# POOL's order of gathers and roots, and two loads moved from the last stage's start into the experts' middle

## The reference

```python
x = x + cross_attention(layernorm(x), ctx, ...)          # 16 heads
x = x + moe(layernorm(x), gate, w_gate, w_up, w_down)    # 64 experts, top 8, 192 hidden
x = x + memory_attention(layernorm(x), ctx, mask)        # softmax(x3 ctx^T / sqrt(512) + mask) ctx
x = x + ffn(layernorm(x), gate_w, up_w, down_w, scales)  # 1408 hidden, ternary weights
```

## Time and profile before

| | |
|---|---|
| median of three runs | 1554.14 us |
| the profiled execution | 1556.91 us, its span 1555.2 us |
| mean granted clock | 0.948 of 2.4 GHz |
| PE busy | 1416.4 us, 91% |
| DVE busy | 1027.0 us, 66% |
| ACT busy | 890.5 us, 57% |
| POOL busy | 609.0 us, 39%, of which L1631 (G gathers) 116.8 us, 112 of them |
| DMA | 278.23 MB, mean 179 GB/s |

### The profile page before, as it was taken

How to read it: one execution, slowest core, us unless ns; L and a number is a source line. 1 busy time by engine, 2 the same in 40 slices (tenths; PEclk the granted TensorE clock), 3 DMA queues, 4 the chain that set the end, 5 groups by cost and what they waited for, 6 DMA issues and landing times.

```text
span 1555.2 us, 37426 instructions
## 1 busy us (share of the span) xinstructions
PE 1416.4 (91%) x8673; PEld 1195.1 (77%) x8674; DVE 1027.0 (66%) x2093; ACT 890.5 (57%) x2022; POOL 609.0 (39%) x698
## 2 busy tenths in 40 slices
PE   7999899999845999999999999999982599999998
PEld 6887666657724898888889888888971488888888
DVE  5555588876687676777676766766645467676742
ACT  5554599873366666666666666766631244444442
POOL 1223387761112322323332323323236566666322
PEclk9999799999955999999999999999995899999999
DMA  6221692001162788878777777777657544444200
GB/s 223 82 88 55 247 359 80 2 5 48 62 250 67 254 277 280 275 252 281 268 266 275 271 256 248 265 243 254 234 162 261 156 149 145 134 135 135 74 13 29
DMA packets 93287, 278.23 MB, mean 179 GB/s; under 512 B 12757, under 2 KB 12886, under 8 KB 92502
## 3 DMA queue, kind: packets, MB, share of 16 engines
q1 hardware_dynamic: 69526, 199.67, 36.6%
q0 software_dynamic: 23680, 77.61, 16.5%
HBM read 209.07 MB, written 76.81 MB: 184 GB/s over the span
## 4 chain that ended last, share of the span: by engine, by line
PE 41%; issue 9%; POOL 5%; DMA 4%; DVE 3%; ACT 3%; ACTq 1%; SPq 1%; DVEq 1%; POOLq 0%
PE m_g L1307 17%; PE m_y L1327 11%; PE f_g L1742 5%; DMA y_rows<-y 2%; PE m_x L1292 2%; POOL G L1631 2%; PE f_y L1757 2%; POOL hT_low L1637 2%; ACT wd_high L1076 1%; PE m_h L1315 1%; PE m_h L1316 1%; PE f_x L1715 1%; DVE X L1796 1%; PE f_sc L1701 1%; DMA raw_gu<-y_rows,slot 1%
## 5 line engine op out<-in xcount | busy, mean ns | idle before, releaser
L1235 POOL DMA_INDIRECT xg<-h_rows,idx x168 | 194.2, 1156 | 454.7 <-PE m_x L1292 445.6
L1307 PE MATMUL m_g<-wgu_high,bxTh 128*128 x660 | 235.8, 357 | 2.3 <-DVE bxTl L1378 2.0
L1307 PE MATMUL m_g<-wgu_low,bxTh 128*128 x660 | 223.3, 338 | 0.0
L1307 PE MATMUL m_g<-wgu_high,bxTl 128*128 x660 | 223.2, 338 | 0.0
L1742 PE MATMUL f_g<-x4T_high,ffn_gu 128*128 128x256 f32 x704 | 176.6, 293 | 4.7 <-DVE x4T_low L1866 4.6
L1742 PE MATMUL f_g<-x4T_low,ffn_gu 128*128 128x256 f32 x704 | 169.8, 283 | 0.0
L1081 DVE TENSOR_TENSOR wgu_low<-raw_gu,wgu_high (+1 forms) x64 | 112.6, 1759 | 85.0 <-ACT wgu_high L1071 80.3
L1378 DVE TENSOR_TENSOR bxTl<-m_x,bxTh 128x512 fp32r<-128x512 f32 x166 | 114.6, 691 | 73.7 <-ACT bxTh L1475 67.5
L1493 ACT ACTIVATE y<-m_y 128x512 f32<-128x512 f32 x164 | 98.3, 600 | 107.1 <-PE m_y L1327 78.3
L1327 PE MATMUL m_y<-wd_high,hidTm 128*128 x328 | 143.9, 439 | 5.9 <-DVE hidTm L1392 3.9
L626 POOL TENSOR_TENSOR prob<-prob,inv 128x512 f32<-128x512 f32 x128 | 130.5, 1042 | 40.1 <-DVE inv L577 38.6
(11 more groups left out here) (266 smaller groups left out, 3291.2 us busy)
## 6 DMA issues: line engine op xcount, KB each, us to landing
raw_gu<-in_exp_gu SPq DMA_DIRECT2D x64, 768.0 KB, 6.4
y_rows<-y SPq DMA_DIRECT2D x164, 256.0 KB
raw_d<-in_exp_d SPq DMA_DIRECT2D x64, 512.0 KB, 7.2
y_rows<-zero SPq DMA_DIRECT2D x64, 256.0 KB, 3.4
ffn_gu<-ffn_gu_words SPq DMA_DIRECT2D x1, 5632.0 KB, 22.0
raw_c<-in_ctxT SPq DMA_DIRECT2D x16, 256.0 KB, 2.7
X<-in_x SPq DMA_DIRECT2D x4, 1024.0 KB, 5.7
h_rows<-h SPq DMA_DIRECT2D x16, 256.0 KB, 2.0
```

Of the source, the lines that this page charges most:

```text
L1235: eng.indirect_dma_start(xg[:, u, :].bitcast(F32), None, h_dram, bass.IndirectOffsetOnAxis(ap=idx[half][:, u:u + 1], axis=0)).then_inc(s_g ...
L1307: m = eng.matmul(pg[u % 2][:, 0:2 * I], xT[l][:, u % 2, c, :], W.gu[r][:, buf * DC + c, :], start=c == 0 and n == 0, stop=c == DC - 1 and ...
```

## The change

Four edits.

1. memT of batch 0 and the mask get places in `spares` (whose other users in the last stage, `xn` and `x3T`, get space of their own) and are loaded by SP in the experts, after group 27, once DVE has ORed the last chunk of words. PE's first scores wait for memT alone, the first read for both halves of the memory.
2. In the last stage SP waits for the early addition k6_1 before it loads mem and the scales. Wdn follows as before.
3. `gather(1, ...)` waits for nothing.
4. POOL's order: three gathers of batch 1, root a of batch 0, the other thirteen, four of batch 2, root 4 of batch 0, five of batch 2, root a of batch 1. The last seven of batch 2 go behind the lows of batch 0, 2, 2, 2 and 1 behind f = 0 to 3, and then eight of batch 3 behind f = 4 to 10 (two behind 10), where there had been eight behind f = 1 to 7.

```diff
 # experts, SP
-                    each_group(eng, begin, groups, stores)
+                    done = WORDS_AT[-1] + 3
+                    with eng.Fori(begin, done) as i:
+                        stores(i)
+                    dveD.wait(eng, FC - 1, "words")
+                    apart(eng, s_apart)
+                    eng.dma_start(memT, a["memT"][:, 0, :, :]).then_inc(s_mem, 16)
+                    eng.dma_start(open8, a["mask"].unsqueeze(0).to_broadcast([P, B, S])).then_inc(s_m, 16)
+                    each_group(eng, done, groups, stores)
 # finish
+    GATHERS_2, GATHERS_3 = {0: 2, 1: 2, 2: 2, 3: 1}, {4: 1, 5: 1, 6: 1, 7: 1, 8: 1, 9: 1, 10: 2}
...
-        xn = spare[0].rearrange("p (i d) -> p i d", i=TPB)
-        x3T = spare[1].rearrange("p (i c n) -> p i c n", i=TPB, c=DC)
+        xn, x3T = sb("xn", [P, TPB, D]), sb("x3T", [P, TPB, DC, P])
 # finish, SP
-            load(0)
-            eng.dma_start(open8[:, :, :], a["mask"].unsqueeze(0).to_broadcast([P, B, S])).then_inc(s_m, 16)
+            added.wait(eng, 0, f"k{K - 2}_{TPB - 1}")
+            apart(eng, s_apart)
+            load(0, True)
 # finish, POOL
-                    if b > 0:
+                    if b > 1:
                         dveA.wait(eng, b - 1, f"k{k}_{i}")
...
-            gather(1, places[:4])
+            gather(1, places[:3])
             deviations_a(0)
-            gather(1, places[4:])
+            gather(1, places[3:])
+            gather(2, places[:4])
             deviations_4(0)
+            gather(2, places[4:9])
             deviations_a(1)
-            gather(2, places)
 
             for b in range(B):
-                n = 0
+                n, of_2, beside = 0, 9, GATHERS if b > 0 else GATHERS_3
                 for f in fs:
                     low(b, f)
+                    if b == 0:
+                        gather(2, places[of_2:of_2 + GATHERS_2.get(f, 0)])
+                        of_2 += GATHERS_2.get(f, 0)
                     if b < B - 1 and f == 7 + (b == 0):
                         deviations_4(b + 1)
                     if b < B - 3:
-                        gather(b + 3, places[n:n + GATHERS.get(f, 0)])
-                        n += GATHERS.get(f, 0)
+                        gather(b + 3, places[n:n + beside.get(f, 0)])
+                        n += beside.get(f, 0)
 # finish, PE
-            def scores(b):
-                eng.wait_ge(s_mem, (b + 1) * 32)
+            def scores(b, first=None):
+                eng.wait_ge(s_mem, first or (b + 1) * 32)
...
             def read(b):
                 actC.wait(eng, b, f"pT{TPB - 1}")
+                eng.wait_ge(s_mem, (b + 1) * 32)
...
-            scores(0)
+            scores(0, 16)
```

More of the change, by code:

```diff
@@ L1125, in norm_scales, with experts @@
     link(eng.scalar_tensor_tensor(lnp[:, :, 1], mv[:, :, 0], -1.0, lnp[:, :, 0], ALU.mult, ALU.mult))
-def experts(nc, block, ctx, h_dram, y_dram, W, Wgu, ffn_d, X, slot8, w8, spares, low_bits, s_ffn, s_over, blk_tok, endb, blk_tab, ident):
+def experts(nc, block, ctx, a, memT, open8, s_mem, s_m, h_dram, y_dram, W, Wgu, ffn_d, X, slot8, w8, spares, low_bits, s_ffn, s_over, blk_tok, endb, blk_tab, ident):
     with ExitStack() as held_here:
@@ L1527, in experts, with finish @@
         return dveE
-def finish(nc, block, ctx, a, out, y_dram, X, spares, spare, slot8, w8, Wgu, ffn_d, low_bits, s_ffn, s_over, added, ident):
+def finish(nc, block, ctx, a, out, y_dram, X, memT, open8, s_mem, s_m, slot8, w8, Wgu, ffn_d, low_bits, s_ffn, s_over, added, ident):
     TI, fs, GUB = range(TPB), range(FC), 3
@@ L1544, in finish @@
         G = sb("G", [P, TPB, K, D])
-        memT, mem = sb("memT_sb", [P, DC, S]), sb("mem_sb", [P, TPB, D])
-        open8, neg, valid = sb("mask_b", [P, B, S], U8), sb("neg", [P, S]), sb("valid", [P, B])
+        mem = sb("mem_sb", [P, TPB, D])
+        neg, valid = sb("neg", [P, S]), sb("valid", [P, B])
         stats, mv, lnp = sb("n_stats", [P, TPB, 6]), sb("n_mv", [P, TPB, 2]), sb("n_lnp", [P, TPB, 2])
         stats4, mv4, lnp4 = sb("n_stats4", [P, TPB, 6]), sb("n_mv4", [P, TPB, 2]), sb("n_lnp4", [P, TPB, 2])
-        xn = spare[0].rearrange("p (i d) -> p i d", i=TPB)
-        x3T = spare[1].rearrange("p (i c n) -> p i c n", i=TPB, c=DC)
+        xn, x3T = sb("xn", [P, TPB, D]), sb("x3T", [P, TPB, DC, P])
         x4T = [sb(f"x4T_{h}", [P, DC, S], F32R) for h in ("high", "low")]
@@ L1561, in finish @@
         ppT = px[0][:, :].rearrange("p (i n) -> p i n", i=TPB)
-        s_g, s_m, s_s, s_apart = [[sem(f"f_g{i}_{k}") for k in range(K)] for i in TI], sem("f_m"), sem("f_s"), sem("f_apart")
-        s_mem, s_o = sem("f_mem"), [sem(f"f_o{i}") for i in TI]
+        s_g, s_s, s_apart = [[sem(f"f_g{i}_{k}") for k in range(K)] for i in TI], sem("f_s"), sem("f_apart")
+        s_o = [sem(f"f_o{i}") for i in TI]
         s_odd, s_sum, s_exact = sem("f_odd"), sem("f_sum"), sem("f_exact")
@@ L1589, in _, with load @@
                 eng.sem_inc(s, 16)
-            def load(b):
-                eng.dma_start(memT[:, :, :], a["memT"][:, b, :, :]).then_inc(s_mem, 16)
+            def load(b, first=False):
+                if not first:
+                    eng.dma_start(memT, a["memT"][:, b, :, :]).then_inc(s_mem, 16)
                 eng.dma_start(mem[:, :, :], a["mem"][:, bass.ts(b, TPB), :]).then_inc(s_mem, 16)
-            load(0)
-            eng.dma_start(open8[:, :, :], a["mask"].unsqueeze(0).to_broadcast([P, B, S])).then_inc(s_m, 16)
+            added.wait(eng, 0, f"k{K - 2}_{TPB - 1}")
+            apart(eng, s_apart)
+            load(0, True)
             eng.dma_start(gs[:, :], a["gate_s"]).then_inc(s_s, 16)
@@ L2058, in build @@
             block = both.enter_context(nc.Block())
-            added = experts(nc, block, both, h_dram, y_dram, W, Wgu, ffn_d, X, slot8, w8, spares, low_bits, s_ffn, s_over, blk_tok, endb, blk_tab, ident)
-        finish(nc, block, both, a, out, y_dram, X, spares, spare, slot8, w8, Wgu, ffn_d, low_bits, s_ffn, s_over, added, ident)
+            memT, open8 = spare[0].rearrange("p (c n) -> p c n", c=DC), spare[1].bitcast(U8)[:, 0:B * S].rearrange("p (b n) -> p b n", b=B)
+            s_mem, s_m = [both.enter_context(nc.semaphore(n)) for n in ("f_mem", "f_m")]
+            added = experts(nc, block, both, a, memT, open8, s_mem, s_m, h_dram, y_dram, W, Wgu, ffn_d, X, slot8, w8, spares, low_bits, s_ffn, s_over, blk_tok, endb, blk_tab, ident)
+        finish(nc, block, both, a, out, y_dram, X, memT, open8, s_mem, s_m, slot8, w8, Wgu, ffn_d, low_bits, s_ffn, s_over, added, ident)
 def lay_out(i):
```

## The result

The changed kernel takes 1544.03 us (1538.61 to 1549.02, eight runs) against 1554.59 (1553.12 to 1559.2) for the kernel before, run beside it: a ratio of 0.9922 [0.9904, 0.994]. It is faster by 9 to 15 us; 19.3 were forecast, and the time lies above the range. The profiled execution took 1545.69 us with a span of 1543.8, 11.4 less than the 1555.2 of before. Two runs further on, one of e1 (1577.97 us) and e7's profiled one (1577.01 us), were slow at a lower clock (0.87 and 0.89), and medians and ratios leave them out.

A forecast was written before the change was run, and what follows sets the result against it. PE was taken to bound the experts and full batches, so only its waits between could shrink: 4.9 + 11.9 + 2.9 + 1.1 - 1.5 = 19.3 us off 1554.14 gave 1534.8 us, range 1530 to 1542.

The forecast's parts named there:

- The early gathers and the first root: Last stage's start: number 15, the last early gather, 4.0 us earlier, normalization 7.7; 4.9 us remain at deviations_4(0).
- Rival (2): Last stage's start: mem, scales and batch 1's first gathers slow numbers 14 and 15; gain 1.3, not 4.9; 1538.4 us, chance 0.12.
- "I take 0" for Wdn: Batch 1's first gathers beside Wdn: scores' chain 1 to 3 us late, costing 0 to 0.3, taken as 0.
- queue term: Between batch 0's two roots: POOL's 17 gathers take 22.3 us and end last, taking back 2.8 of 7.7 us.
- "I take 0" for the middle loads: Experts' middle, near 965 us: memT and mask, 768 KB, cost 0; under 1 us if they delayed a store.
- The 11.9 us: Batch 0: PE's wait before the transposes of the probabilities, behind POOL's sixteen gathers of batch 2, goes whole: 11.9 us.
- the slow stretch behind it: Batch 0: matmuls and transposes behind PE's long wait run at the full clock again, 2.9 us gained.
- Rival (3): Batch 0: PE waits in pieces from f 3, clock held near 1.2 GHz until batch 1; 1559.8 us, chance 0.02.
- rival (4): Start gives nothing; low 3 or ACT's table loads keep half of the 11.9 us; about 9 gained, 1545, chance 0.04.
- "1.1 us" at the end of batch 0: End of batch 0: the 0.84 us DVE kept PE, plus 0.3 for smaller waits, counted as 1.1 us gained.
- Rival (1): Gathers beside DVE cost 1.5 to 1.7 us each, 2.6 of it in low 3 to low 10; 1542.1 us, chance 0.13.
- Batch 1's turn: Start of batch 1: root behind six gathers, not four; PE waits 1.5 us (0 to 2.5) for normalized rows.

The follow-up runs named there:

- e1: Changed kernel without the two loads in the experts' middle (memT of batch 0 and the mask never loaded): 1543.16 us, ratio 0.991 to the kernel before.
- e7: e6 with the two loads in the experts' middle cut in four, behind groups 28 to 31: 1551.83 us, ratio 0.9977 to the kernel before.
- e2: Changed kernel with Wdn's load held until DVE's fifth addition of batch 1: 1545.18 us, ratio 0.9926 to the kernel before.
- e3: Changed kernel with two, not four, gathers of batch 3 between batch 0's last low and deviations_a(2): 1541.38 us, ratio 0.9895 to the kernel before.
- e11: Changed kernel with Wdn's load moved behind load(1) and behind the last addition of batch 1: 1541.66 us, ratio 0.9901 to the kernel before.
- e12: Changed kernel with a third DMA of 768 KB ahead of the two loads in the experts' middle: 1545.74 us, ratio 0.9936 to the kernel before.
- e5: Changed kernel with Wdn's load held until batch 1's last addition, load(1) behind it: 1551.79 us, ratio 0.9972 to the kernel before.
- e9: e6 with load(1) (memT and mem of batch 1) ahead of Wdn on SP's queue: 1533.66 us, ratio 0.9852 to the kernel before.
- e10: e9 with the two loads in the experts' middle cut in quarters behind groups 28 to 31: 1537.26 us, ratio 0.9881 to the kernel before.
- e4: Kernel before with POOL's new order alone, all of SP's loads where they were: 1543.61 us, ratio 0.9918 to the kernel before.
- e8: Changed kernel's loads with POOL's old order: 1554.05 us, ratio 0.9991 to the kernel before.
- e6: Changed kernel with Wdn after batch 1's last addition, fewer gathers before POOL's roots, none of batch 3's at f 8 to 10: 1551.33 us, ratio 0.9974.

## Why the prediction was wrong in its size

The sign and the mechanism of the large term were right. What failed is the pricing of the moves' side effects: two terms that the sum puts at 0 (the moved loads' place in the experts and Wdn beside the gathers) and two that it made too favourable (the end of batch 0, batch 1's turn). Together they are 7.9 us of the span. The median, 1544.03, lies 2.0 above the range's end.

**The early gathers and the first root: right.** Number 15 comes 4.1 us earlier against the `y` copy (4.0 forecast), the root 7.6 (7.7). That it fits to 0.1 is luck: in the other kernels with the same program there (e1, e2, e3, e11, e12) number 15 comes 3.0 to 5.3 us earlier. Rival (2) is refuted: number 15 did not slow down beside mem and the scales.

**"I take 0" for Wdn: the failed step of the start, 1.4 of its 1.6 us.** The prediction gave the gathers beside Wdn the old 7 to 9 us and POOL 2.8 us of slack. Brought together with more gathers, the one at 1182.90 took 11.6 us and the next 10.0, and DVE waited 2.16 and 1.62 us. First root to `deviations_4(0)` took 25.0 us, not 23.6. So the moments, not POOL's queue, ended last, which the prediction had named as the sign of a wrong queue term; e11, without those waits, takes 23.2, so the price of the queue was right; e11's gain at the root, 4.3 us, is just under the 4.4 to 5.9 allowed, since its first root is 0.8 late. The term is shown by e2, e5 and e11 together; e2 shows also that a Wdn a little later only stalls other gathers. The Trainium skill, "DMA: Bandwidth & Descriptors", section "Queues, rings and completion order", says that a DMA engine takes turns between the queues it has work for, packet by packet. The traces agree in kind: the third gather lands after 11.4 to 12.4 us in the four traces with Wdn right behind it and after 5.3 to 6.0 in the four where it comes later (e2, e9, e10, e11), and Wdn itself takes 13.0 us, not the 10.2 of before.

**"I take 0" for the middle loads: the largest miss, 3.1 us later at the last `y` copy, 2.7 of it in the loads' stretch.** I took as evidence the window with 512 KB of down words. Its neighbours were the same, 1280 KB of weights in front and the `y` stores behind, and its loads were not free: ACT waited 1.23 us for its `y` buffer, which cost PE nothing. With 768 KB ACT waited 3.8 us and PE 1.71. So a full busy time of PE hid a delay of the stores that was just short of reaching PE, and half as many bytes again passed that point. The bound "under 1 us" priced SP's issues and the transfer's own time, not the stores behind it, and it forgot the slow clock behind PE's pause. By the table of 112 to 128 the loads cost 0.5 to 2.4 us in a trace, 1.7 on the mean, and e12 shows the cost following the bytes. The other 0.4 of the 3.1 is not explained, and the end of the experts scatters by more than that between traces without these loads: 1162.21 before, 1162.04 in e4, 1166.65 in e1.

**The 11.9 us and the slow stretch behind it: right.** The wait is gone, low 2 waits for ACT and not for gathers, `f_hid` waits at most 1.9 us for a low, and the clock is 1.00 around 1250. e4 and e8 show that POOL's order does it, alone. Rival (3), the clock, and rival (4) are refuted; that rival (4)'s 1545 lies 1 us from the measured time is chance, for the start gave 3.3 us and the long wait went whole.

**"1.1 us" at the end of batch 0: 1.4 us too much.** The 0.84 us of the earlier trace rows went, but low 10 now stands behind gathers of batch 3, and PE's down words wait 1.12 us for it at 1253.70. Rival (1) had this wait in it at 2.6; gathers beside DVE did take up to 1.59 us, as at 1224.78, but not as a rule: the 112 of L1644 take 0.97 us at the median and 1.06 on the mean. In e9, with no gather at f 8 to 10, there is no such wait, and batch 0 takes 42.9 us, with 42.7 forecast.

**Batch 1's turn: the wait right, its price too small.** I said 1.5 us; PE waited 1.83, and 2.0 with all that followed. What I missed is the clock: 1.4 us more in the executions in which it fell. The prediction had priced a slow clock behind the long wait and in rival (3), and not behind its own wait of 1.5. e3, without the wait, has neither loss.

With these the forecast's 19.3 becomes 19.3 - 1.6 - 3.1 - 1.4 - 1.8 = 11.4, the difference of the spans. It closes because the four are the table's own differences; the experiments, not the sum, show their causes, and for the middle loads they show 1.7 of the 3.1 on the mean.

## What to carry to other kernels

Price a transfer that is moved by how late it makes what stands behind it on its queue, and by how much lateness the engine that counts can take. A window in which that engine stays busy does not say the transfer is free: the engine in between already waited 1.2 us there, and a transfer half as large again cost time. Order one queue by when each landing is needed: load(1) behind Wdn lost what the other edits of e6 had won, and its swap with Wdn (e6 to e9) brought 17.7 us between the medians (13.2 between the spans of the two profiles). Where PE is to wait even 1.8 us, add the slow clock behind it to the bad end of the range.

## What was not expected of the hardware

- The same wait of 1.83 to 1.87 us at the same place was followed by a clock at 0.50 for 3 to 4 us in five kernels (changed, e1, e2, e5, e12) and by none in two (e4, e11). Why these two are spared was not settled. The Trainium skill, "TensorE: Matmul & The Clock Gate", section "Part 1: The HAM clock gate (the "warmup" mystery)", says that the number of slow matmuls at a kernel's start differs from run to run of one kernel. A like chance behind a wait would fit, but no run here tests it. The 1.12 us wait at 1252.6 was followed by none, here and in the seven other traces that have it; nor were PE's pauses of 1.3 to 1.5 us in the experts' middle of e2, e8 and e11, while the changed kernel's 1.71 us there was. In e6, pauses of 0.90, 0.20 and 1.12 us within 3 us were followed by a clock at 0.50.
- A 256 KB gather issued just ahead of a 2816 KB load on another queue landed after 11.6 us, three times its time alone and twice the 5.3 us that it took in e11 with only mem and the scales beside it. The load took 13.0 us, against 10.2 in the kernel before.
